# Expert choice in three parts of 16 experts, two of them beside the experts' products

## The chip, the cores and the metric

The kernel is one launch on one core of a Trainium2 chip. The metric is the device time of the launch in microseconds. The engines are TensorE (PE), VectorE (DVE), ScalarE (ACT), GpSimd (POOL) and SyncE (SP); the last one only issues transfers. All data are fp32.

## The reference, cut to what matters

Two layers over x of 4 x 1024 rows of 256. Layer 0 is a gated attention and a mixture of 48 experts with expert choice, layer 1 a performer encoder and a feed-forward net. The part that matters here, with T = 4096 rows, E = 48 experts and S = 4 blocks each:

```python
cap = int(1.5 * T / E)                    # 128
logits = xf @ Wr.T                        # T x E
vals, idx = jax.lax.top_k(logits.T, cap)  # 128 best rows for each expert
w = jax.nn.softmax(vals, axis=-1)
h = jax.nn.gelu(jnp.einsum('ecd,esdm->ecsm', xf[idx], W1) + b1[:, None], approximate=False)
y = jnp.einsum('ecsm,esmk->ecsk', h, W2) + b2[:, None]
out = zeros.at[idx.reshape(-1)].add(y * w)
```

Layer 1 needs, beside its inputs, two weights folded with the random features (Wk and Wq times proj), and constants: ln1_b @ W1, the column sums of W2, and shift @ W1 of the last net.

## The kernel before

The stages run one after the other, each in a block of its own; inside a block every engine has its own instruction list, and semaphores set the order between engines. The function `expert_choice` has three blocks.

**The logits stage** (L633 to L768, 100 to 150 us). Eight groups (n) of 512 rows. VectorE updates x, takes statistics (POOL the reciprocal root) and the shift; ScalarE normalises into z; TensorE turns z; ScalarE modulates (`modulate`); TensorE turns back and ScalarE copies the rows (`rows`, L716) into hg, which SP writes to h_dram (L641). TensorE multiplies with Wr, and VectorE's `logits_copy` (L678) puts 48 x 512 logits into `logits`, two groups of 48 partitions with 2048 columns each. On VectorE `logits_copy(n - 2)` stands behind `statistics(n + 1)`; hg and the logits in PSUM have two buffers each.

**The choice** (L770 to L932). VectorE does 16 rounds over `logits` (112 x 2048): MAX8, FIND_INDEX8 and MATCH_REPLACE8 (L825 to L828), eight values a round. Each expert then has two descending lists of 128. TensorE turns both and flips one, and VectorE takes the larger of each pair, which are the 128 best; index and weight follow. Beside this SP loads the first 8 experts and small columns, and TensorE and ScalarE make the two folds (16 transposes L899, a copy, 32 instructions of products L904, a copy L874, a store), the weights of which are loaded in this block, and the three constants (L912, L915, L919).

**The products** (L935 to L1102). A ring of 8 experts' weights. For expert e TensorE does up(e + 1) (32 instructions, L1082), turn(e + 2) of the gathered rows (L1073) and down(e) (16, L1091). VectorE adds b1 over 128 x 1024 (L1053) and b2 (L1064), ScalarE copies the turned rows (L1023), does one GELU over 128 x 1024 (L1027) and weighs y (L1032). POOL gathers rows six experts ahead (L987) and adds y to a sum in DRAM (L999). SP loads expert e + 8 once b2 of e has been added. All run in loops of eight experts.

Of the kernel before, what the change touches and what calls it, by code (L numbers as in the profile page):

```python
# [12 lines left out]
ALU = mybir.AluOpType  # L13
# [4 lines left out]
I32 = mybir.dt.int32  # L18
# [570 lines left out]
TOP = 8  # L589


def expert_choice(nc, mk, g, a):

    HALF = T // 2
    LOW = 64
    ROWS = LOW + E
    with ExitStack() as ctx:
# [6 lines left out]
        weight = t.sb("weight", [P, E])  # L604
        h_dram = nc.dram_tensor("h_dram", (T, D), F32, kind="Internal").ap()
# [10 lines left out]
        with ExitStack() as c2:  # L616
            r = Maker(nc, c2)
            logits = r.sb("logits", [ROWS, HALF])

            with ExitStack() as c3:  # L620
                t = Maker(nc, c3)
                z, hg = t.sb("z", [P, 2, G, D]), t.sb("hg", [P, 2, G, D])
                hT = t.sb("hT", [P, 2, KD, GT])
                wrT = t.sb("wrT", [P, KD, E])
                st, mv, var, rstd, shift = (t.sb("st1", [P, G, 6]), t.sb("mv1", [P, 2, G, 2]), t.sb("var1", [P, 2, G]), t.sb("rstd1", [P, 2, G]),
                                            t.sb("shift1", [P, 2, G]))
                tp, lp, back = t.ps("tp1", [P, 2, KD, GT]), t.ps("lp1", [P, 2, GT]), t.ps("back1", [P, G, D])
                own, blank, var_ready, rstd_ready, shift_ready = (mk.sem("ec_dve"), mk.sem("ec_blank"), mk.sem("ec_var"), mk.sem("ec_rstd"),
                                                                  mk.sem("ec_shift"))
                z_ready, turned, hT_ready, back_done, h_ready = (mk.sem("ec_z"), mk.sem("ec_turned"), mk.sem("ec_hT"), mk.sem("ec_back"),  # L630
                                                                 mk.sem("ec_h"))
                logits_done, logits_out, wrT_done, wrT_copied = (mk.sem("ec_logits"), mk.sem("ec_logits_out"), mk.sem("ec_wrT"),
                                                                 mk.sem("ec_wrT_copied"))  # L633
                h_out = [mk.sem("ec_h_out0"), mk.sem("ec_h_out1")]
                part = lambda n: slice(LOW * (n // (NG // 2)), LOW * (n // (NG // 2)) + E)
                with nc.Block() as block:
                    @block.sync
                    def _(sp):
                        for n in range(NG):
                            sp.wait_ge(h_ready, n + 1)  # L640
                            sp.dma_start(h_dram[n * GT:(n + 1) * GT, :].rearrange("(t p) d -> p t d", p=P), hg[:, n % 2]).then_inc(h_out[n % 2], 16)  # L641
                        for k in range(2):
                            sp.wait_ge(h_out[k], 16 * (NG // 2))

                    @block.gpsimd
                    def _(pool):
                        pool.memset(logits[32:64, :], LOWEST).then_inc(blank, 1)
                        pool.wait_ge(blank, 1)
                        for n in range(NG):
                            pool.wait_ge(var_ready, n + 1)  # L650
                            if n >= 2:
                                pool.wait_ge(shift_ready, n - 1)
                            rsqrt_rows(pool, rstd[:, n % 2], var[:, n % 2], g.minus_half, G, rstd_ready)

                    @block.vector
                    def _(dve):
                        v = Steps(dve, own)

# [1734 lines left out]
```

## Time and profile before

| | |
|---|---|
| time, three runs | 1721.37, 1722.84, 1730.1 us, median 1722.84 |
| the profiled execution | 1728.49 us, its span 1726.7 us |
| TensorE busy in the span | 1495.2 us, 87% |
| VectorE | 1171.5 us, 68% |
| ScalarE, POOL | 642.8 us and 526.5 us, 37% and 30% |
| granted TensorE clock, mean | 0.924 of full |

Shares over the whole span mix stages with different limits: one reads the stretch that a change touches. Busy times overlap across engines. The span begins with the first and ends with the last instruction of the profile, and the rest of the execution's time lies around it.

### The profile page before, as it was taken

Reading aid. Unit: us, or ns where it says so; the run is one execution under the profiler, and the core shown is the slowest. Engines: PE = TensorE matmul, PEld = TensorE weight load, DVE = VectorE, ACT = ScalarE, POOL = GpSimd, SP = SyncE. Lnnn points to the kernel's source line nnn. Section 1 sums busy time; section 2 is a strip of 40 time slices with the busy share of each in tenths; the row PEclk is TensorE's granted clock in tenths of the full one; section 3 lists DMA queues with packets and bytes.
Section 4 is the critical chain, followed back from the end, with each engine's and each line's share of the span. In section 5 each row is a group of like instructions: output and inputs, shape, how many; then the busy total and the mean of one; then the engine's idle time right before and its main releaser. Section 6 shows DMA issues by size and latency. Waiting matters only on the chain. (4 is left out here: it accounts for less than half of the span.)

```text
span 1726.7 us, 22918 instructions
## 1 busy us (share of the span) xinstructions
PE 1495.2 (87%) x8460; PEld 1248.3 (72%) x8460; DVE 1171.5 (68%) x1867; ACT 642.8 (37%) x947; POOL 526.5 (30%) x511
## 2 busy tenths in 40 slices
PE   8874236999998399999997999999976999989997
PEld 6442236999998266666655788888865888878887
DVE  6576992222222668877737878787856987798886
ACT  1044102333333122222222333333326776766774
POOL 2410003555554012222224200000003555546666
PEclk7788657999999599999998999999997999999999
DMA  5516903999993301112113000000012100000001
GB/s 195 220 37 235 320 6 98 296 292 297 297 291 58 123 25 37 37 37 62 36 49 110 0 25 25 25 25 25 13 52 98 50 25 14 1 1 25 13 25 37
DMA packets 127835, 157.16 MB, mean 91 GB/s; under 512 B 13952, under 2 KB 95992, under 8 KB 126720
## 3 DMA queue, kind: packets, MB, share of 16 engines
q1 hardware_dynamic: 115952, 138.12, 24.6%
q0 software_dynamic: 9216, 12.59, 3.6%
q10 hardware_dynamic: 2576, 5.26, 0.8%
q8 instruction: 54, 0.88, 0.2%
q14 instruction: 37, 0.30, 0.1%
HBM read 122.35 MB, written 33.60 MB: 90 GB/s over the span
## 5 line engine op out<-in xcount | busy, mean ns | idle before, releaser
L2031 POOL TENSOR_TENSOR ff_hid_lo<-ff_hid,ff_hid_hi 128x512 fp32r<-128x512 f32 x128 | 176.0, 1376 | 161.1 <-ACT ff_hid_hi L1940 161.1
L1082 PE MATMUL h_ps<-xT,w 128*128 128x128 f32 x1536 | 192.9, 284 | 1.0 <-ACT xT L1023 1.0
L1082 PEld LDWEIGHTS h_ps<-xT,w 128*128 128x128 f32 x1536 | 186.3, 197 | 1.6 <-issue 0.9
L1053 DVE TENSOR_TENSOR pre<-h_ps,b1T 128x1024 f32<-128x1024 f32 x48 | 58.8, 1225 | 176.4 <-PE h_ps L1082 176.4
L2315 PE MATMUL ff_down<-ff_w_hi,ff_hid_hi 128*128 128x256 f32 x512 | 147.7, 288 | 4.1 <-POOL ff_hid_lo L2031 3.6
L2317 PE MATMUL ff_down<-ff_w_hi,ff_hid_lo 128*128 128x256 f32 x512 | 146.4, 286 | 0.0
L2316 PE MATMUL ff_down<-ff_w_lo,ff_hid_hi 128*128 128x256 f32 x512 | 146.2, 286 | 0.0
L116 POOL TENSOR_TENSOR ff_rstd<-ff_var,minus_half 128x4 f32<-128x4 f32 x24 | 25.5, 1061 | 358.9 <-DVE ff_var L111 356.6
L1117 PE MATMUL k_ring<-w_hi,hT_hi 128*128 128x512 f32 x256 | 118.7, 464 | 9.5 <-DVE hT_lo L1277 6.4
L1458 PE MATMUL k_acc<-wide_rows,hk 128*128 128x512 f32 x256 | 119.7, 599 | 4.3 <-ACT wide_rows L1402 4.3
L1117 PE MATMUL q_ring<-w_hi,hT_hi 128*128 128x512 f32 x256 | 109.8, 429 | 9.8 <-PEq L99 6.8
L1747 PE MATMUL q_out_ps<-kv_sums,wide_rows 128*128 128x256 f32 x512 | 115.5, 379 | 0.0
L2301 PE MATMUL ff_ring<-ff_rowsT_hi,ff_w_hi 128*128 128x512 f32 x256 | 103.0, 402 | 8.4 <-DVE ff_rowsT_lo L2089 3.6
L2315 PEld LDWEIGHTS ff_down<-ff_w_hi,ff_hid_hi 128*128 128x128 f32 x512 | 99.1, 194 | 10.6 <-POOL ff_hid_lo L2031 5.0
L1747 PEld LDWEIGHTS q_out_ps<-kv_sums,wide_rows 128*128 128x128 f32 x512 | 96.3, 190 | 13.2
L2302 PE MATMUL ff_ring<-ff_rowsT_lo,ff_w_hi 128*128 128x512 f32 x256 | 102.4, 400 | 0.0
L2316 PEld LDWEIGHTS ff_down<-ff_w_lo,ff_hid_hi 128*128 128x128 f32 x512 | 99.3, 194 | 4.2
L1119 PE MATMUL k_ring<-w_hi,hT_lo 128*128 128x512 f32 x256 | 102.2, 399 | 0.0
L1118 PE MATMUL k_ring<-w_lo,hT_hi 128*128 128x512 f32 x256 | 101.8, 398 | 0.0
L1119 PE MATMUL q_ring<-w_hi,hT_lo 128*128 128x512 f32 x256 | 101.7, 397 | 0.0
L1118 PE MATMUL q_ring<-w_lo,hT_hi 128*128 128x512 f32 x256 | 101.6, 397 | 0.0
L1393 ACT ACTIVATE k_squares<-k_ring 128x1024 f32<-128x1024 f32 x32 | 32.8, 1025 | 182.3 <-PE k_ring L1119 182.3
(374 smaller groups left out, 3537.4 us busy)
## 6 DMA issues: line engine op xcount, KB each, us to landing
w<-in_L_ffn_W_dram SPq DMA_DIRECT2D x48, 1024.0 KB, 5.8
w<-in_L_ffn_W_dram SPq DMA_DIRECT2D x48, 256.0 KB, 6.1
expert_sum_dram<-f_zero SPq DMA_DIRECT2D x8, 1024.0 KB, 14.9
b_rows<-in_L_ffn_b_dram SPq DMA_DIRECT2D x48, 128.0 KB, 8.8
x<-in_L_attn_x_dram SPq DMA_DIRECT2D x4, 1024.0 KB, 12.4
h_dram<-hg SPq DMA_DIRECT2D x8, 512.0 KB, 2.9
hk<-expert_sum_dram SPq DMA_DIRECT2D x8, 512.0 KB, 4.4
hT_hi<-expert_sum_dram SPq DMA_DIRECT2D x8, 512.0 KB, 5.2
```

The source lines that it names most:

```text
L1082: last = pe.matmul(h_ps[:, q % 2, s * KD + c, :], w1[:, q, s, k, c::KD], xT[:, q % 2, k, :], start=(k == 0), stop=(k == KD - 1))
L1117: pe.matmul(out, x[0], w[0][:, cols], start=start, stop=False)
L1118: pe.matmul(out, x[0], w[1][:, cols], start=False, stop=False)
L1119: return pe.matmul(out, x[1], w[0][:, cols], start=False, stop=stop)
L1458: last = pe.matmul(acc[:, k, cols], hk[:, n % KV_RING, j, k * P:(k + 1) * P], dash[:, n % 2, j, cols], start=(j == 0), stop=(j == G - 1))
L1747: last = pe.matmul(out_ps[:, i % 2, 0:D], qnT[:, i % 2, c, :], kv_out(i // TB)[:, c, :], start=(c == 0), stop=(c == CH - 1))
L2031: pool.tensor_tensor(hid_lo[:, m % PARTS, :], hid[:, m % WHOLES, :], hid_hi[:, m % PARTS, :].bitcast(F32), ALU.subtract).then_inc(part_low, 1)
L2301: pe.matmul(slot(u), high[:, d, cols], x[:, n % 2, d, :], start=(d == 0), stop=False)
L2302: pe.matmul(slot(u), high[:, d, cols], x_low[:, n % 2, d, :], start=False, stop=False)
L2315: pe.matmul(into, hid_hi[:, m % PARTS, tile], high[:, c, :], start=(c == 0 and j % 2 == 0), stop=False)
L2316: pe.matmul(into, hid_hi[:, m % PARTS, tile], low[:, c, :], start=False, stop=False)
L2317: last = pe.matmul(into, hid_lo[:, m % PARTS, tile], high[:, c, :], start=False, stop=(c == CF - 1 and j % 2 == 1))
```

## The change

- The experts are chosen in three parts of 16 (`PHASES`). The logits of part p lie in `lists[:, p, :]`, 128 partitions x 512: partition 16 n + i holds expert i of the part over the rows of group n. Each part takes 16 rounds over 128 x 512, gives 8 descending lists of 128 for each expert, and finds the 128th value by merging them as bitonic lists on 16 partitions (`send_lists`, `sort_steps`), without indices. Then the lists' entries above that value are counted, their places found by a product with triangles (`rank`), and indices and weights are moved to them by seven conditional shifts (`move`) and joined by products.
- Part 0 runs before the first product, and the first 8 rounds of part 1 too. The rest of part 1 and part 2 are cut into slots behind `add(e)` on VectorE, with their TensorE steps ahead of `down(e)`. Iterations 0 to 3 and 12 to 19 have two rounds each, iterations 4 to 13 and 20 to 29 the merging.
- The logits go through `stage` and three transfers a group (`spread`) to their partitions.
- In the logits stage SP also loads the weights of folds and constants (1 MB each, into ring slots 3 to 7), and experts 0 and 1. Choice and products are one block, so two blocks are left.
- b1 becomes the bias of eight GELUs of 128 x 128; VectorE's addition is gone. The loops are unrolled. Rows are gathered 5 experts ahead. x_ps and y_ps take one bank each, and `down(e)` waits for `add(e - 1)`. The sums over W2 are made by POOL (seven additions) and one product.

```diff
+PHASES = 3
+EP = E // PHASES
+LISTS = P // EP
+AHEAD, STARTS, ROUND_SLOTS, COUNTS_AT = 8, (0, 0, 12), (0, 4, 8), (0, 8, 24)
+FOLD_SLOT, ELU_SLOT, WAVE_SLOT = 3, 5, 7
...
+                    def ahead(n):
+                        if n == 0:
+                            for k in range(2):
+                                sp.dma_start(proj2[:, k, :], a["L1_attn_proj"]).then_inc(proj_in, 16)
+                        if n < 2:
+                            sp.dma_start(w_raw[n], a[("L1_attn_Wk", "L1_attn_Wq")[n]]...).then_inc(fold_in[n], 16)
...
+                        if 5 <= n < NG - 1:
+                            load_expert(sp, n - 5, n - 5)
+                    def spread(n):
+                        sp.wait_ge(logits_out, n + 1)
+                        for i in range(PHASES):
+                            sp.dma_start(lists[n * EP:(n + 1) * EP, i, :], stage[i * EP:(i + 1) * EP, n % 2, :]).then_inc(lists_in[n % 2], 16)
+                    for n in range(NG):
+                        sp.wait_ge(h_ready, n + 1)
+                        sp.dma_start(h_dram[n * GT:(n + 1) * GT, :]..., hg[:, n % 2]).then_inc(h_out[n % 2], 16)
+                        ahead(n)
+                        if n >= 2:
+                            spread(n - 2)
...
+                    def logits_copy(n):
+                        dve.wait_ge(logits_done, n + 1)
+                        if n >= 2:
+                            dve.wait_ge(lists_in[n % 2], 16 * PHASES * (n // 2))
+                        dve.tensor_copy(stage[:, n % 2, :], lp[0:E, n % 2, :]).then_inc(logits_out, 1)
...
-                        act.activation(act_h[:, q % 2], pre[:, q % 2], ACT.Gelu).then_inc(gelu_done, 1)
+                        for s in range(S):
+                            for c in range(KD):
+                                last = act.activation(act_h[:, e % 2, s * KD + c, :], h_ps[:, e % 2, s * KD + c, :], ACT.Gelu,
+                                                      bias=b1T[:, e * S + s, c:c + 1])
...
+                    def sort_steps(lists_left, first, count):
+                        for i in range(first, first + count):
+                            j = P >> (i + 1)
+                            of, to = (order[:, (i + x) % 2, 0:lists_left, :]... for x in range(2))
+                            v.mark(dve.tensor_tensor(to[:, :, 0, :], of[:, :, 0, :], of[:, :, 1, :], ALU.max))
+                            v.mark(dve.tensor_tensor(to[:, :, 1, :], of[:, :, 0, :], of[:, :, 1, :], ALU.min))
+                            v.sync()
...
+                    def move(lists, first, count):
+                        for i in range(first, first + count):
+                            of, to, step = lists[:, i % 2, :], lists[:, (i + 1) % 2, :], 1 << i
+                            v(dve.tensor_scalar(to, of, bits[:, 1, i:i + 1], None, ALU.mult))
+                            v(dve.scalar_tensor_tensor(to[:, step:], of[:, 0:P - step], bits[:, 0, i:i + 1], to[:, step:], ALU.mult, ALU.add))
...
+                    rounds(0, 0, CAP // TOP)
+                    listed(0)
+                    turn_back(0)
+                    first_level(0)
+                    sort_steps(4, 0, 7)
+                    second_level()
+                    sort_steps(2, 0, 7)
+                    last_level()
+                    counts(0)
+                    placed(0)
+                    move(moved, 0, 7)
+                    dve.sem_inc(shifted, 1)
+                    weights_in(0)
+                    indices(0)
+                    move(moved_w, 0, 7)
+                    dve.sem_inc(valued, 1)
+                    rounds(1, 0, AHEAD)
+                    weights(0)
+                    for e in range(E):
+                        add(e)
+                        for p in range(1, PHASES):
+                            k = e - STARTS[p]
+                            if 0 <= k < ROUND_SLOTS[p]:
+                                rounds(p, CAP // TOP - 2 * (ROUND_SLOTS[p] - k), 2)
+                            if k == ROUND_SLOTS[p] - 1:
+                                listed(p)
+                            if e == COUNTS_AT[p] - 4:
+                                turn_back(p)
...
+                    for e in range(E):
+                        if e + 1 < E:
+                            up(e + 1)
+                        if e + 2 < E:
+                            turn(e + 2)
+                        for p in range(1, PHASES):
+                            if e == COUNTS_AT[p] - 4:
+                                turn_top(p)
+                            if e == COUNTS_AT[p] - 3:
+                                send_lists(p)
+                            if e == COUNTS_AT[p] + 1:
+                                rank(p)
+                            if e == COUNTS_AT[p] + 3:
+                                join_indices(p)
+                            if e == COUNTS_AT[p] + 5:
+                                join_weights(p)
+                        down(e)
```

The rest of the slots: `first_level` with three sorting steps behind add(5), four and `second_level` behind add(6), seven and `last_level` behind add(7), `counts` behind add(8), `placed` and three shifts behind add(9), four behind add(10), `indices`, `weights_in` and four shifts behind add(11), three behind add(12), `weights` behind add(13); for part 2 the same 16 experts later. Before the first product TensorE's list is turn_top(0), send_lists(0), the third constant, send_edge(0), rank(0), join_indices(0), join_weights(0), turn(0), up(0).

## Rows read from the trace of the kernel before

**Rows 1.** windows of two stretches: busy us of each engine, TensorE's clock, DMA share, GB/s.
```profile
150.00:270.00 120.00, 35.38 (x189) 32.49 (x189) 113.47 (x93) 8.73 (x10) 0.61 (x3) 0.61 0.52 180
...
300.00:400.00 100.00, 100.00 (x867) 100.00 (x866) 28.11 (x35) 33.77 (x53) 54.70 (x87) 1.00 1.02 295
```

**Rows 2.** timeline of VectorE, two starts of a round: start us, duration us, instruction.
```profile
150.20 2.29 DVE L825 MAX8 top<-logits 112x8 f32<-112x2048 f32 x1 [1.90 <-PEq L636]
...
157.31 2.29 DVE L825 MAX8 top<-logits 112x8 f32<-112x2048 f32 x1
```

**Rows 3.** groups of VectorE by shape: busy us, mean ns of one, idle before.
```profile
L1053 DVE TENSOR_TENSOR pre<-h_ps,b1T 128x1024 f32<-128x1024 f32 x48 | 58.8, 1225 | 176.4 <-PE h_ps L1082 176.4
...
L1064 DVE TENSOR_TENSOR biased_y<-y_ps,b_rows 128x256 f32<-128x256 f32 x48 | 20.4, 425 | 32.1 <-PE y_ps L1091 32.1
...
L678 DVE COPY logits<-lp 48x512 f32<-48x512 f32 x8 | 5.5, 689 | 13.8 <-PE lp L741 13.7
...
L315 DVE TENSOR_TENSOR masked<-coef,eye_b 128x128 f32<-128x128 f32 x2 | 0.6, 292 | 0.1
```

**Rows 4.** timeline from the last round to the first product.
```profile
262.94 0.39 DVE L833 COPY both<-rank_ps 128x224 f32<-128x224 f32 x1 [0.79 <-PE rank_ps L924]
...
263.45 0.66 PE L927 MATMUL peak_ps<-both,rank 128*128 128x48 f32 x2 [0.54 <-DVEq L834]
...
271.32 1.29 POOL L987 DMA_INDIRECT xg<-h_dram,slot  x1 [0.46 <-POOL pool_spare L980]
...
274.53 0.70 PE L1073 MATMUL x_ps<-ident,xg 128*128 128x128 f32 x2 [5.64 <-DMA xg<-h_dram,slot]
...
275.80 0.55 PE L1082 MATMUL h_ps<-xT,w 128*128 128x128 f32 x1 [0.56 <-ACT xT L1023]
```

**Rows 5.** timeline of TensorE, two neighbouring experts.
```profile
334.13 3.99 PE L1082 MATMUL h_ps<-xT,w 128*128 128x128 f32 x32
...
339.91 3.99 PE L1082 MATMUL h_ps<-xT,w 128*128 128x128 f32 x32
```

**Rows 6.** timeline at the second expert's down().
```profile
291.94 1.90 PE L1091 MATMUL y_ps<-w,act_h 128*128 128x64 f32 x16
```

**Rows 7.** timeline of the logits stage.
```profile
121.25 2.07 ACT L699 ACTIVATE z<-x,shift,rstd 128x256 f32<-128x256 f32 x4
...
123.22 1.00 ACT L716 ACTIVATE hg<-back 128x1024 f32<-128x1024 f32 x1
...
125.55 0.68 DVE L678 COPY logits<-lp 48x512 f32<-48x512 f32 x1 [0.17 <-PE lp L741]
```

**Rows 8.** DMA issues of the whole span: count, KB each, us from issue to landing.
```profile
w<-in_L_ffn_W_dram SPq DMA_DIRECT2D x48, 1024.0 KB, 5.8
...
b_rows<-in_L_ffn_b_dram SPq DMA_DIRECT2D x48, 128.0 KB, 8.8
...
xg<-h_dram,slot POOLq DMA_INDIRECT x48, 5.5
...
ff_b_elu<-in_L_attn_b_dram SPq DMA_DIRECT2D x1, 4.0 KB, 12.0
...
ff_wav<-in_L_ffn_b_dram SPq DMA_DIRECT2D x1, 4.0 KB, 2.6
```

**Rows 9.** timeline of one fold pass.
```profile
188.80 3.67 PE L899 MATMUL fold_ps<-ident,w_raw 128*128 128x128 f32 x16 [13.69 <-DMA w_raw<-in_L_attn_Wq_dram]
...
199.70 1.88 ACT L874 ACTIVATE w_fold<-fold_ps 128x2048 f32<-128x2048 f32 x1 [5.30 <-PE fold_ps L904]
```

**Rows 10.** groups of ScalarE by shape.
```profile
L1032 ACT ACTIVATE y<-biased_y,weight 128x256 f32<-128x256 f32 x48 | 24.4, 508 | 6.1 <-DVE biased_y L1064 2.6
L1023 ACT ACTIVATE xT<-x_ps 128x256 f32<-128x256 f32 x48 | 18.4, 383 | 149.9 <-PE x_ps L1073 149.9
...
L699 ACT ACTIVATE z<-x,shift,rstd 128x256 f32<-128x256 f32 x32 | 16.6, 592 | 1.1 <-DVE shift L672 1.1
...
L1027 ACT ACT_TABLE_LOAD x1 | 1.3, 1283 | 0.0
```

More of the change, by code:

```diff
@@ new lines, in _, with carry, scatter @@
+                    steps = iter(range(1, 3 * E))
+                    def carry():
+                        carry_wait(next(steps))
+                    def scatter(e):
+                        pool.wait_ge(y_ready, e + 1 + 2)
+                        carry()
+                        pool.indirect_dma_start(out=sums[e % 2], out_offset=bass.IndirectOffsetOnAxis(ap=slot[:, e % XG], axis=0),
+                                                in_=y[:, e % 2, :], in_offset=None, compute_op=ALU.add).then_inc(added[e % 2], 16)
@@ L1047, in _, with exps @@
-                    bodies(act, body)
+                        act.activation(y[:, e % 2, :], biased_y[:, e % 2, :], ACT.Copy, scale=weight[:, e:e + 1]).then_inc(y_ready, 1)
+                    def exps(p):
+                        act.wait_ge(edge_ready, p + 1)
+                        act.activation(ex[:], top[:], ACT.Exp, bias=edge[:, 1:2]).then_inc(top_exp, 1)
+                    act.wait_ge(fold_turned, 1)
+                    act.wait_ge(blank, 1)
+                    for i in range(2):
+                        rows = slice(i * DH, (i + 1) * DH)
+                        last = act.activation(features[rows, i * MF:(i + 1) * MF], fold_ps[rows, 0:MF], ACT.Copy, scale=DN)
@@ L1050, in _ @@
                 def _(dve):
[L1051 to L1061 removed]
+                    v = Steps(dve, own)
@@ new lines, in rounds, with listed @@
+                    def rounds(p, first, count):
+                        for n in range(first, first + count):
+                            cols = slice(n * TOP, (n + 1) * TOP)
+                            v(dve.max(top[:, cols], lists[:, p, :]))
+                            v(dve.max_index(at[:, cols], top[:, cols], lists[:, p, :]))
+                            if n < CAP // TOP - 1:
+                                v(dve.match_replace(lists[:, p, :], top[:, cols], lists[:, p, :], LOWEST))
+                    def listed(p):
+                        dve.sem_inc(found, 1)
+                        v(dve.tensor_copy(at_f[:], at[:]))
@@ new lines, in _ @@
+                    turn_top(0)
+                    send_lists(0)
+                    pe.wait_ge(wave_w_in, 16)
+                    for c in range(CF):
+                        for k in range(KD):
+                            last = pe.matmul(fold_ps[:, 1024 + c * B:1024 + (c + 1) * B], w_wave[:, k, c * P:(c + 1) * P], g.shift_col[:, k, :],
+                                             start=(k == 0), stop=(k == KD - 1))
+                    last.then_inc(wave_consts, 1)
+                    send_edge(0)
```

825 lines of the change are left out of this document (440 added, 385 removed).

## The prediction

> **What bounds the kernel now.** I read the windows by stage first. Between the logits and the experts' products lie 120 us in which VectorE works 113 us, TensorE a third of the time and at half clock for much of it. That is the choice. From 300 us on, the products keep TensorE at 100.00 of 100 us at full clock, with the DMA engines at their limit too (share 1.02) [rows 1]. So in the choice only VectorE counts, and in the products only TensorE. The timeline of the choice shows a round: three passes over 112x2048, 7.11 us from one MAX8 to the next, 2.37 us a pass with its gap [rows 2]. There are 16 rounds, without the last MATCH_REPLACE: 47 passes or 111.4 us, from 150.2 to 261.6 us. From there to the first product (275.80 us) 14.2 us go by, in handshakes, the stage's end and the first gather [rows 4]. In the products one expert takes 5.78 us [rows 5].
>
> The sum below is made against the span, 1726.7 us; that execution took 1728.49 us, 5.7 us above the median 1722.84. The difference is taken off the median.
>
> **1. Shorter passes before the first product.** Each partition now holds 512 logits instead of 2048, and only a third of the experts has to be chosen first. The trace shows no MAX8 of 512. Two VectorE passes out of PSUM, 256 and 512 columns wide, take 425 and 689 ns, 1.03 ns a column [rows 3]; 1536 columns fewer make 2.37 into 0.79 us. 47 passes: 37.1 us, 74.3 us less. Bounds: a quarter of 2.37 (no fixed cost) gives 27.8 us, 0.9 us a pass 42.
>
> **2. A longer way from the last round to the first product.** The lists of 8 partitions must be merged. From the end of the rounds, F: transpose and turn back 1.4 us (the exchange with TensorE costs 0.79 [rows 4]); eight products of a 16-column list with 128 columns, 16 instructions, between 0.33 us (0.66 for two that stand alone, cold [rows 4]) and 0.125 (warm, part 4), I take 0.24, 4.0; first level 1.6 (689 + 2 x 425 ns); seven sorting steps of two 256-column operations, 0.9 each, 6.3; second level 0.6; seven steps of two 128-column ones (292 ns [rows 3]), 0.63 each, 4.4; last level 1.0; the edge through TensorE 0.8; counts 1.2; ranks 1.1; 14 small operations of placed() at 0.17 to 0.2 us, 3.0; 14 of move() over 128 columns at 0.29, 4.0; join_indices 0.8, the copy 0.2. Indices at F + 30.4. The gather adds 0.9 to its issue and 3.2 to landing (271.32 to 274.53 [rows 4]). But join_weights stands ahead of turn(0) on TensorE, and waits for a second move() of 4.0: turn(0) at F + 35.5, up(0) at F + 36.8. Against 14.2: +22.6 us. If TensorE is warm and short operations overlap, +17; if each handshake costs 0.5 more, +28.
>
> **3. The logits stage.** Beside each h block, SP now issues 1 MB of weights (two experts, 1.4 MB each, at n = 5 and 6), and then three transfers of spread(n - 2). logits_copy(n) waits for these on VectorE, and behind it stand update, statistics and shift of the following blocks, for which ScalarE waits. In the trace logits_copy(2) starts at 125.55, while rows(2) has just ended at 124.22 [rows 7]; only then can h, weights and spread(0) be issued. When does spread land? A 4 KB load took 12.0 us behind others and 2.6 us on an empty queue; 1 MB takes 5.8 us, a broadcast of b2 8.8 us [rows 8]. I take it that spread lands behind its neighbours: 6.3 us after rows(n), 10 after an expert's load. Step by step: copy(2) at 131 instead of 125.6; shift(5) 5.7 us late; R(4), the end of rows(4), at 136.8 instead of 133.5; copy(4) at 143; R(5) at 141.4; copy(5), behind expert 0's b2, at 152; copy(6), behind expert 1's, at 158; spread(7) issued by 161.4 and landed by 163.5. The first MAX8 starts there instead of at 150.2: +13.3 us. If small transfers land in 2.6 us, +6.4; if SP's issues are held up by a full queue as well, +20. The Trainium skill ("DMA: Bandwidth & Descriptors", Why a DMA increments its semaphore by 16 and not by 1 and the section on ordering of hardware queues) says that a completion increment lands only after every earlier write of that DMA engine. By it the stage costs the 13.3; without it the 6.4. The row of the 4 KB load agrees with it.
>
> Off the path: the weights of the folds are in place when the choice starts. One fold pass took 12.8 us (188.80 to 201.58 [rows 9]), so two, the projection and the constants take some 35 us from 161.7 and end 3 us before the rounds (200.6). POOL's seven sums replace eight products and are done by then. If the rounds come out shorter, this chain takes their place. In the loops the hardware queue loses nothing: the same 1.4 MB an expert.
>
> **4. The products.** The bias leaves VectorE (58.8 us in all [rows 3]) and becomes part of eight GELUs of 128x128. Neither was on the path, so nothing is gained. TensorE gains instructions, and it is the bound: per later part 1 transpose, 16 for the lists, and 2, 4, 2 and 4, 29 at 0.125 us (3.99 us for 32 [rows 5]), 3.6 us; two parts 7.2. The rest is waits. y_ps now lies in one bank, so down(e) waits for add(e-1), which stands behind VectorE's rounds. Before the loop VectorE does 8 rounds of part 1 (19.0 us) and weights(0), so add(0) ends at F + 54.6. down(1) would start 16.1 us after up(0) (291.94 - 275.80 [rows 4, 6]), at F + 52.9: 1.8 us. Each slot then has two rounds, 4.74 us, and add, 0.42: 5.2 of 5.78, which fits. turn_top(1) in iteration 4 waits for the end of slot 3: TensorE is ready at F + 72.8, the list at F + 75.1, 2.5 us. In part 2 the same wait is 5.3 - 4.3 = 1.1 us. An Exp in iterations 8 and 24 brings two table loads of 1.28 us [rows 10] into ScalarE; GELU is then 0.4 us late, 0.8 in all. Sum: 7.2 + 1.8 + 2.5 + 1.1 + 0.8 = 13.4 us. Gathers five ahead have over two experts' time, 11.6 us, to land, and land in 5.5 [rows 8], so LEAD costs nothing. Unrolled loops: TensorE has no idle time between 300 and 400 us, where two passes of the loop of eight experts end [rows 1], so nothing is gained. The Trainium skill ("Runtime: NRT & Kernel Launch", Instruction fetch mechanics) says that a taken branch can cost a fetch and straight code none; by it the loop would win something. The full window speaks against a gain here.
>
> **Sum.** -74.3 + 22.6 + 13.3 + 13.4 = -25.0 us: the median goes to 1697.8, I say 1698.
>
> **The rivals.**
> - Spread lands in 2.6 us whatever is in the queue (the other 4 KB row): the stage costs 6.4 instead of 13.3, 1691 us. Chance 0.20.
> - The products lose more: every expert 0.3 us longer because add and turn_top hang on VectorE's slots with 0.6 us of room. 48 x 0.3 = 14.4: 1712 us. For it: 5.2 of 5.78 is an estimate over unseen passes (rounds of 2.65 us fill the slot). Against: between two down() TensorE has 5.78 - 1.90 = 3.9 us of other work [rows 5, 6], in which add may be late. Chance 0.16.
> - The folds end after the rounds: rounds at the lower bound (27.8 us) would end at 191.3, the constants at 197; TensorE then sets the start, 1694 us. Chance 0.06.
> - Slower than before: ScalarE becomes the bound of the products. It does one copy (383 ns), weigh (508 ns) [rows 10] and eight GELUs of g. With 0.5 us of gaps, 5.78 us are full at g = 0.55 us; at 0.72, 7.15 us an expert, the loop loses 66 us: 1763. It decides against the change from g = 0.64 on. For it: a 128x256 pass with scale and bias takes 592 ns on the average [rows 10]. Against: four of them lie within 2.07 us [rows 7], so 0.52 each, and half the columns cost less; I take 0.32. Chance 0.05.
> - The change does what it says and no more is late: the rest.
>
> **How the numbers follow.** My forecast 0.53 (own range 1688 to 1708), the others as above. The median of this kernel can be told from no change from about 0.5% on, 8.6 us. Faster: the forecast, the first and third rival, and two thirds of the second: 0.53 + 0.20 + 0.06 + 0.09 = 0.88; same 0.07; slower 0.05. The range leaves out the best bounds (all at once -55 us) and the slower case: 1680 to 1713.
>
> **What the profile would show.** MAX8 128x512 at 0.7 us; first MAX8 near 163 us; up(0) near 237 us; logits copies with waits for DMA of some 5 us; an expert still 5.78 us; TensorE idle before turn_top. Wrong I am most likely in the logits stage (spread's landing) and in the count of small steps after the rounds.

## The result, and the profile after

The changed kernel takes 1698.22 us (median of 4 runs, 1696.27 to 1701.64), the kernel before in the same comparison 1722.57 us: ratio 0.9846, 95% interval 0.982 to 0.9873. The forecast was 1698. Measured in the traces, its four terms sum to -28.1 us instead of -25.0, with errors of 0.9 to 3.3 us in each.

The timeline of the changed kernel at the borders of its stages (columns as in [rows 2]: start, duration, engine, line, operation, and in brackets the idle time before it and its releaser):

```profile
97.43 1.40 DVE L105 BATCH_NORM_STATS2 st<-x 128x6 f32<-128x256 f32 x4 [1.42 <-PEq L99]
...
163.05 0.69 DVE L995 MAX8 top<-lists 128x8 f32<-128x512 f32 x1
...
165.37 0.69 DVE L995 MAX8 top<-lists 128x8 f32<-128x512 f32 x1
...
167.68 0.70 DVE L995 MAX8 top<-lists 128x8 f32<-128x512 f32 x1
...
199.37 0.47 PE L1172 MATMUL pick_ps<-ident,top 128*128 128x128 f32 x1 [8.32 <-DVEq L1001]
...
234.60 6.58 PE L1214 MATMUL h_ps<-xT,w 128*128 128x128 f32 x32 [0.56 <-ACT xT L934]
...
525.77 0.42 DVE L1105 TENSOR_TENSOR biased_y<-y_ps,b_rows 128x256 f32<-128x256 f32 x1 [2.15 <-PE y_ps L1225]
```

A round takes 2.31 us (165.37 to 167.68) instead of 7.11, and the line of turn_top says that TensorE, done with its folds, idled 8.32 us for VectorE. By such starts the two traces compare as follows (us; the span of the changed kernel is 1694.5, its clock 0.934):

| stage | before | after | difference | forecast |
|---|---|---|---|---|
| up to the first BN_STATS of the logits stage | 100.35 | 97.43 | -2.9 | 0 |
| logits stage, to the first MAX8 | 49.85 | 65.62 | +15.8 | +13.3 |
| 47 passes | 111.4 | 36.2 | -75.2 | -74.3 |
| last round to up(0) | 14.2 | 35.3 | +21.2 | +22.6 |
| products, up(0) to the last add | 281.1 | 291.2 | +10.1 | +13.4 |
| the rest | 1169.8 | 1168.7 | -1.1 | 0 |

The spans differ by 32.2 us, the medians by 24.35. The 7.9 us between are scatter: the profiled execution of the kernel before took 5.9 us more than its median, that of the changed kernel 1.95 us less. Of them 2.9 lie in the first row, a stage that both kernels share (looked at in experiment 1).

**The logits stage.** Answers for the logits copy and the list transfers of the changed kernel (the second figure in "26.1, 6" is the number of waits):

```profile
L708 DVE COPY logits_rows<-lp x8: 682/683/683, 112.5 to 158.6; 48x512 f32<-48x512 f32 x8
  DMA lists<-logits_rows: 26.1, 6
L664 SPq DMA_DIRECT2D lists<-logits_rows x24: 507/592/1160, 121.5 to 160.9; - x24
DMA to landing us min/median/max: 1.9/5.3/6.3
```

VectorE stood 26.1 us in six waits for lists. The last h copy (hg) ends 52.4 us after the first BN_STATS; in the kernel before it was 46.4. So the waits behind which update, statistics and shift stood cost 6.0 us. The other 9.8 us lie behind that copy: 13.2 us to the first MAX8 instead of 3.4. SyncE's queue in the changed kernel shows them:

```profile
145.96 0.37 SPq L668 DMA_DIRECT2D h_dram<-hg  x1
146.37 0.51 SPq L615 DMA_DIRECT2D w<-in_L_ffn_W_dram  x1
146.92 0.90 SPq L616 DMA_DIRECT2D w<-in_L_ffn_W_dram  x1
147.87 0.94 SPq L617 DMA_DIRECT2D b_rows<-in_L_ffn_b_dram  x1
148.84 2.46 SPq L664 DMA_DIRECT2D lists<-logits_rows  x3
151.35 0.58 SPq L668 DMA_DIRECT2D h_dram<-hg  x1
151.97 9.48 SPq L664 DMA_DIRECT2D lists<-logits_rows  x9
```

The last h block is issued at 151.35, 1.5 us after its copy ended, for SP is still busy with expert 1 and spread(4). The last row merges three spreads, and a wait lies inside it. VectorE's copy of block 6, the last six issues in a narrower window, and SP's waits from 145 to 165 us (total, times, longest):

```profile
157.07 0.68 DVE L708 COPY logits_rows<-lp 48x512 f32<-48x512 f32 x1 [7.25 <-DMA lists<-logits_rows]
...
157.78 3.67 SPq L664 DMA_DIRECT2D lists<-logits_rows  x6
...
SPq L664 <- DVE logits_rows L708: 4.6, 2, 3.5
```

So three issues take 2.26 us, then SP waits 3.5 us for the copy of block 6, which itself waited 7.25 us for its staging buffer, that is for the landing of spread(4); the last six issues take 3.67 us.

**The products.** TensorE's timeline around expert 4 of the changed kernel:

```profile
263.76 1.90 PE L1225 MATMUL y_ps<-w,act_h 128*128 128x64 f32 x16
...
270.68 0.33 PE L1172 MATMUL pick_ps<-ident,top 128*128 128x128 f32 x1 [0.98 <-DVEq L1001]
270.84 1.91 PE L1225 MATMUL y_ps<-w,act_h 128*128 128x64 f32 x16
272.59 3.99 PE L1214 MATMUL h_ps<-xT,w 128*128 128x128 f32 x32
...
276.73 0.39 PE L1178 MATMUL pick_ps<-ident,topT 128*16 128x128 f32 x2
...
278.27 0.38 PE L1178 MATMUL pick_ps<-flip,topT 128*16 128x128 f32 x2
278.58 2.00 PE L1225 MATMUL y_ps<-w,act_h 128*128 128x64 f32 x16
```

From down to down one expert takes 7.08 us (263.76 to 270.84, with the wait of 0.98 for VectorE's rounds), the next 7.74 (16 list instructions), an expert without side work 5.78 as before [rows 5]. From 300 to 400 us, TensorE works 99.70 of 100 us (it was 100.00 [rows 1]).

### The profile page after: what moved, and what is told of

Its sections match the earlier page's. It is cut to its first block and busy times, and to the rows that moved or that the text cites. A ratio compares the mean times of both kernels' runs of the same rounds, so it can differ in the third digit from the quotient of the medians.

```text
span 1694.5 us, 23216 instructions
## 1 busy us (share of the span) xinstructions
PE 1501.0 (89%) x8521; PEld 1251.7 (74%) x8521; DVE 1175.3 (69%) x2242; ACT 694.1 (41%) x1289; POOL 533.4 (31%) x519
## 5 line engine op out<-in xcount | busy, mean ns | idle before, releaser
L1105 DVE TENSOR_TENSOR biased_y<-y_ps,b_rows 128x256 f32<-128x256 f32 x48 | 20.4, 425 | 148.0 <-PE y_ps L1225 137.0
L2501 PEld LDWEIGHTS ff_down<-ff_w_hi,ff_hid_hi 128*128 128x128 f32 x512 | 98.6, 193 | 11.2 <-POOL ff_hid_lo L2217 5.0
L1933 PEld LDWEIGHTS q_out_ps<-kv_sums,wide_rows 128*128 128x128 f32 x512 | 96.3, 190 | 13.2
L940 ACT ACTIVATE act_h<-h_ps,b1T 128x128 f32<-128x128 f32 x384 | 104.0, 390 | 2.8 <-PE h_ps L1214 2.7
## 6 DMA issues: line engine op xcount, KB each, us to landing
expert_sum_dram<-f_zero SPq DMA_DIRECT2D x8, 1024.0 KB, 15.4
```

What stands on the lines that cost most here:

```text
L940: last = act.activation(act_h[:, e % 2, s * KD + c, :], h_ps[:, e % 2, s * KD + c, :], ACT.Gelu, bias=b1T[:, e * S + s, c:c + 1])
L1933: last = pe.matmul(out_ps[:, i % 2, 0:D], qnT[:, i % 2, c, :], kv_out(i // TB)[:, c, :], start=(c == 0), stop=(c == CH - 1))
L2501: pe.matmul(into, hid_hi[:, m % PARTS, tile], high[:, c, :], start=(c == 0 and j % 2 == 0), stop=False)
```

## The experiments

Times are medians. The kernel before was timed again beside each group of runs, and its median came out between 1722.57 and 1724.83 us, so kernels of different groups are best compared by their ratios. "Stage" is from the first BN_STATS to the first MAX8, "products" from up(0) to the last add, both as in the table.

**1. The kernel before once more.**

> The kernel before, unchanged, profiled a second time. Its first profiled execution took 1728.49 us, 5.9 us over its median, and reached the first BN_STATS of the logits stage 2.9 us later than the changed kernel did, in a stage that the change doesn't touch. Theory: that is scatter between executions, so this one shows the logits stage from some 97.5 us on, a logits stage of 49.9 us and products of 281 us again, and a time near 1722. Rival: the change moves the stage in front too (its layout in memory, its instruction stream); then the stage starts at 100.3 again, whatever the time.

1727.2 us for this one execution, beside a median of 1722.91. First BN_STATS at 100.61, logits stage 49.1, products 281.7. The stages repeat within 0.8 us, so the table's differences hold to about that. The start of the stage is the rival's (100.3), not the theory's (97.5), but the rival's reason doesn't hold for every kernel either: of the twelve profiles of the changed kernel and its variants below, ten have their first BN_STATS between 96.9 and 98.1 us and two at 100.2. The front stage thus has two lengths some 2.7 us apart, and the changed kernel's family shows both; the kernel before was seen at the long one twice. Whether it also has the short one stays open, and so does the place of the other 5 us of scatter.

**2. The logits stage: who makes the lists late?** Four edits of the changed kernel.

```
e1_spread_first
-                        ahead(n)
                         if n >= 2:
                             spread(n - 2)
+                        ahead(n)
e2_stage4
-            stage = t.sb("logits_rows", [E, 2, GT])
+            stage = t.sb("logits_rows", [E, 4, GT])
-                        if n >= 2:
-                            dve.wait_ge(lists_in[n % 2], 16 * PHASES * (n // 2))
+                        if n >= 4:
+                            dve.wait_ge(lists_in[n % 4], 16 * PHASES * (n // 4))
e3_no_ahead
-                        ahead(n)
+                    (start of the next block: the same loads, experts 0 to 2, then the columns)
e11_spread_pool
-                            spread(n - 2)      (on SP)
+                        if n >= 3:
+                            spread(n - 3)      (on GpSimd, behind rsqrt_rows of block n)
```

> The changed kernel, but SP issues the three transfers of spread(n - 2) ahead of the weights of block n, not behind them. Theory (a list lands behind the loads that were issued before it): each list then follows only the 0.5 MB h block and lands about 4 to 5 us after R(n), the end of the h copy, instead of 8 to 11; the logits copies wait 1 to 2 us each instead of up to 7.3, the stage takes 54 to 58 us instead of 65.6, and the time is some 10 us under 1698: 1688. Rival (SP's own issue times and a fixed latency of some 5 us set the landing): only the issue of one or two loads, 1 to 2 us, goes; the stage takes 63 to 64 us and the time is 1696.

> The changed kernel with four staging buffers for the logits instead of two, so that logits_copy(n) waits for spread(n - 4) and not for spread(n - 2). Theory (the wait of VectorE for the lists holds back update and statistics behind it): spread(n - 4) has landed by the time of the copy, the waits go, R(7) falls from 149.9 to about 140 us on the clock of the changed kernel, and the last lists still land behind expert 1's load: stage 55 to 58 us, time 1689. Rival (the stage is held by the DMA engines, which move 5 MB of weights and 4 MB of h in it): h writes and lists come as late as before, ScalarE waits for the h buffers in place of VectorE for the lists, and the stage stays at 63 to 66 us, time 1697.

> The changed kernel, but all weights for folds, constants and the experts 0 and 1 are issued at the start of the next stage instead of in the logits stage. Theory: without them the logits stage takes about 53 us (three small lists a block remain), 12 us less; the fold chain starts some 5 us after the stage begins, at 157, and takes 35 us; it ends at about 192, 5 us behind the rounds (187), so 7 to 8 of the 12 us are kept: 1690. Rival (the loads were not what made the stage long; the lists' own latency was): the stage takes 62 us or more, and the later fold chain makes it slower than the changed kernel: 1700 or more.

> The changed kernel, but the lists are sent from GpSimd's queue instead of SP's; loads, buffers and everything else as they are. Theory (a list lands late because it stands behind 1 MB of weights in the same queue): from a queue of its own it lands 2 to 2.5 us after its issue, the copies wait less than 2 us each, the h copies end 47 us after the first BN_STATS and the stage takes 54 to 56 us: 1687. Rival (all queues share the 16 DMA engines, which the loads keep full, so another queue doesn't help): lists land 5 us after their issue as before, and the stage takes 62 us or more: 1695 or more.

| run | us | ratio to before, interval | stage | to the end of the last h copy | from there to MAX8 | list, issue to landing (median) |
|---|---|---|---|---|---|---|
| changed kernel | 1698.22 | 0.9846 (0.982 to 0.9873) | 65.6 | 52.4 | 13.2 | 5.3 |
| e1_spread_first | 1694.73 | 0.9841 (0.9815 to 0.9867) | 61.3 | 48.4 | 12.9 | 3.9 |
| e2_stage4 | 1688.27 | 0.9793 (0.9775 to 0.9811) | 57.5 | 46.4 | 11.2 | 4.8 |
| e3_no_ahead | 1698.97 | 0.9866 (0.9845 to 0.9888) | 55.1 | 47.0 | 8.1 | 2.4 |
| e11_spread_pool | 1688.21 | 0.9788 (0.9773 to 0.9803) | 56.5 | 45.4 | 11.1 | 5.0 |

By their ratios e2 and e11 are faster than the changed kernel, while e1 and e3 can't be told from it by the time (the intervals overlap).

The last column answers the question of the landing. Without loads a list lands 2.4 us after its issue, with them 5.3: the loads cost 2.9 us a list. But my account of how was wrong. From GpSimd's own queue, which carries no weights, the list lands after 5.0 us too. GpSimd's timeline in this run, and the answer for its transfers' line:

```profile
126.73 1.51 POOL L673 DMA_DIRECT2D lists<-logits_rows  x3
...
136.01 1.44 POOL L673 DMA_DIRECT2D lists<-logits_rows  x3 [3.13 <-DVE logits_rows L708]
140.66 1.43 POOL L673 DMA_DIRECT2D lists<-logits_rows  x3 [3.21 <-DVE logits_rows L708]
144.14 1.44 POOL L673 DMA_DIRECT2D lists<-logits_rows  x3 [2.05 <-DVE logits_rows L708]
```

```profile
DMA to landing us min/median/max: 3.1/5.0/6.4
```

So most of the delay is not the place in SP's queue; what both queues share are the DMA engines. Two findings on SP's own queue fit this: the changed kernel's last six lists, issued from 157.8 us on with the DMA share at 0.17, landed after 1.9 to 2.0 us, and with the lists issued ahead of their block's load (e1) the median was 3.9. One thing stays open: a list from GpSimd without the loads was not run. Its shortest landing was 3.1 us, against 1.9 on SP, so a part of the 5.0 may be that queue's own. The engines are busier in this stage than before it was changed; windows of the changed kernel (PEclk, DMA share and GB/s at the end):

```profile
120.00:130.00 10.00, 7.65 (x40) 3.78 (x38) 3.00 (x14) 6.26 (x10) 1.01 (x1) 1.00 1.01 347
140.00:150.00 10.00, 6.89 (x36) 3.47 (x35) 1.43 (x3) 6.90 (x10) 0.00 (x0) 1.00 0.99 287
```

The same windows of the kernel before have shares of 0.34 and 0.37. Yet the run from GpSimd's queue had a landing of 5.0 and lost all waits of the copies. What it changed is when a list is issued: SP's program held spread(n - 2) behind its wait for h block n, though its copy was long done (copy(0) ended at 113.2, spread(0) went out at 121.5), and each of the three issues costs SP 0.5 to 1.2 us. The list waits were thus SP's order, plus its issue times, plus a landing lengthened by the loads; one long link less was enough. The rival was right on the landing and wrong on the time. The Trainium skill ("DMA: Bandwidth & Descriptors", Issuing engines are not separate DMA queues) says both halves of this: transfers from any engine run on the same DMA engines, and another issuing engine saves only the time of issuing, which it calls small beside the transfer. The runs agree on the first half. On the second, the issues were not small here: the three of a block took SP 2.0 to 2.9 us, beside a landing of 5.3. In this run the stage's end is set by something else. SP had issued the last h block by 144.2, expert 1's 1.4 MB just ahead of it, and then waited for the h writes; the next block began at 152.50:

```profile
SPq L666 <- DMA h_dram<-hg: 7.8, 1, 7.8
```

Four buffers take back all 6.0 us of the first part and 2.0 of the second; stage and time came as forecast, though the last h copy was forecast to come 10 us earlier. SP's nine last issues now follow each other without a wait:

```profile
149.90 6.17 SPq L664 DMA_DIRECT2D lists<-logits_rows  x9
```

Spread first got 4.3 us, between the two forecasts: a list still goes out only behind the wait for h(n). How long the copies wait says little by itself. Their waits sum to 26.1, 21.7 and 15.3 us in the changed kernel, e1 and e3, and the last h copy came 6.0, 2.0 and 0.6 us later than in the kernel before.

**3. Why does the run without loads gain nothing?** It shortened the stage by 10.5 us, more than the other three, and took 1698.97 us. Its queue and TensorE:

```profile
175.44 0.67 SPq L617 DMA_DIRECT2D b_rows<-in_L_ffn_b_dram  x1
176.16 1.91 SPq L854 DMA_DIRECT2D ff_b_elu<-in_L_attn_b_dram  x1
178.10 6.46 SPq L856 DMA_DIRECT2D ff_ln_col<-in_L_attn_ln_g_dram  x1
...
190.62 0.58 SPq L862 DMA_DIRECT2D ff_wav<-uantum_weights_imag_dram  x1
```

```profile
173.43 3.84 PE L1251 MATMUL h_ps<-features,w_turned 128*128 128x128 f32 x32 [1.97 <-ACT w_turned L967]
193.78 6.96 PE L1259 MATMUL h_ps<-ff_ln_col,w 128*128 128x1 f32 x32 [16.51 <-issue]
...
201.60 0.42 PE L1178 MATMUL pick_ps<-ident,top 128*128 128x128 f32 x1
```

The folds were done at 177. The constants, which stand ahead of turn_top(0) on TensorE, then waited 16.51 us. The row names no releaser, but the wait ends 2.6 us after SP issued the last of the column loads, which stood behind 4.2 MB of experts. The rounds were over at 188.8 (152.57 + 36.2), turn_top came at 201.6. I tested that by the order alone:

```
e10_columns_first (against e3_no_ahead)
-                    for e in range(FOLD_SLOT):
-                        load_expert(sp, e, e)
                     ... (column loads)
+                    for e in range(FOLD_SLOT):
+                        load_expert(sp, e, e)
```

> The run without loads in the logits stage once more, but the small column loads are issued ahead of the experts 0 to 2, not behind them. Theory (there the constants waited until 193.8 us for columns queued behind 4.2 MB of experts, and TensorE reached turn_top 12.8 us after the rounds' end): the constants end before the rounds do, turn_top follows the rounds at once, up(0) comes 71.6 us after the first MAX8 again, and the time is 12 us less than there: 1687. Rival (the folds' own weights are late too, or the experts' weights now come after up(0) is ready): half of that, 1692 or more.

1689.61 us, ratio 0.98 (0.9785 to 0.9815), 9.4 us less than the run before by the medians and 11 by the ratios, of 12 forecast; stage 55.8. turn_top came at 194.40, still 4.6 us behind the rounds (153.62 + 36.2 = 189.8), instead of 12.8. The order of the queue was the main cause. The rest is TensorE's: its fold products took 6.75 and 6.71 us here instead of 3.84, at a mean granted clock of 0.61 from 159 to 191 us (0.82 in the run above; why it was lower isn't shown). This is the third rival of the prediction, the folds that end after the rounds, seen at work.

It was closer than one profile of the changed kernel says. The run with six gathers (e4, below) changes nothing in this stretch; its products of the folds took 6.78 and 6.74 us at a mean granted clock of 0.59 (166 to 203 us), and of the cover of 8.32 us this was left:

```profile
202.56 0.47 PE L1172 MATMUL pick_ps<-ident,top 128*128 128x128 f32 x1 [0.90 <-DVEq L1001]
```

**4. The products.** Four edits:

```
e4_lead6
-            XG, LEAD = 8, 5
+            XG, LEAD = 8, 6
e5_bias_dve
-       for s, c: act.activation(act_h[:, e % 2, s * KD + c, :], h_ps[:, e % 2, s * KD + c, :], ACT.Gelu, bias=...)
+       act.activation(act_h[:, e % 2], act_h[:, e % 2], ACT.Gelu)
+       dve, ahead of add(e): act_h[:, (e + 1) % 2] = h_ps[:, (e + 1) % 2] + b1T, 128x1024
e6_no_side_work
-       rounds, listed, ... weights of p = 1, 2 and TensorE's and ScalarE's steps for them
-       index[:, e:e + 1], weight[:, e:e + 1]
+       index[:, e % EP:e % EP + 1], weight[:, e % EP:e % EP + 1]
e7_pe_order
-       join_weights(0); turn(0); up(0); turn(1)          -       turn_top(p); down(e)
+       turn(0); up(0); join_weights(0); turn(1)          +       down(e); turn_top(p)
```

> The changed kernel with six gathers ahead again instead of five (LEAD = 6). Theory (a gather has two experts' time and more to land, and lands in about half of it, so its lead costs nothing): products 291 us, 1698, the ratio to before as that of the changed kernel, 0.985. Rival (the fifth gather came too late for some expert, and part of the 10 us that the products grew is a wait of TensorE for a gather): the products shrink by 1 to 3 us. Against six: gather(16) would stand in GpSimd's queue before index 16 exists, and could hold the scatter of expert 11; that would show as one longer interval near expert 12, at most 2 us.

1697.68 us, ratio 0.9838 (0.981 to 0.9866), products 291.2. Lead costs nothing, at five or six.

> The changed kernel without the choice of parts 1 and 2: the experts 16 to 47 take the indices and weights of the experts 0 to 15, so rounds, sorting, lists and moves of two thirds of the experts are left out, and so are TensorE's 58 instructions for them. Theory (all of the 10.1 us that the products grew is side work: TensorE's own instructions and its waits for VectorE): the products take 281 us again, 5.78 us each, and the time is 1688. Rival (gathers five ahead, the split GELU or the unrolled loops cost something by themselves): an interval stays over 5.78 us, and the products take 284 us or more.

1685.92 us for one execution of this kernel, which leaves out the choice of parts 1 and 2; products 281.5, and every interval 5.78 but the last two. So unrolled loops, the lead and the split GELU cost nothing, and win nothing: of the 10.1 us that the products grew, 9.65 are side work (291.17 - 281.52).

> The changed kernel with the bias b1 back on VectorE: one addition of 128x1024 an expert (1.22 us, 58.8 us in all) ahead of each add, and one GELU of 128x1024 in place of eight of 128x128. Theory (in the 12 slots with rounds VectorE has 5.1 us of work in 5.78, so it can't take 1.22 us more; outside of them the bias costs nothing): the 12 slots take 6.4 to 7 us instead of 5.8 to 7, which is 5 to 12 us more in the products, none after expert 20; 1706. Rival (the chain up, bias, GELU, down is longer than the 3.9 us that TensorE has between two downs when VectorE is in a round): each of the 12 slots waits for a whole round more, 2.3 us, 28 us in all: 1726, slower than before. Third (VectorE has the room): 1698.

1720.87 us, ratio 0.9975 (0.9961 to 0.999): almost the whole gain of the change is gone. Products 314.2, 23 us more, nearer to the rival in size, but neither theory had the place. VectorE and TensorE of this run:

```profile
243.45 1.22 DVE L1102 TENSOR_TENSOR act_h<-h_ps,b1T 128x1024 f32<-128x1024 f32 x1 [8.88 <-PE h_ps L1221]
244.59 0.68 DVE L993 MAX8 top<-lists 128x8 f32<-128x512 f32 x1
...
263.60 1.22 DVE L1102 TENSOR_TENSOR act_h<-h_ps,b1T 128x1024 f32<-128x1024 f32 x1
264.75 0.41 DVE L1109 TENSOR_TENSOR biased_y<-y_ps,b_rows 128x256 f32<-128x256 f32 x1
```

```profile
253.83 0.39 PE L1212 MATMUL x_ps<-ident,xg 128*128 128x128 f32 x2
265.97 3.68 PE L1232 MATMUL y_ps<-w,act_h 128*128 128x64 f32 x16 [11.76 <-ACT act_h L940]
269.44 5.74 PE L1221 MATMUL h_ps<-xT,w 128*128 128x128 f32 x32
```

bias(1) stands behind eight rounds: the first two intervals take 15.0 us more, 11.76 of them the wait, the rest a down of 3.68 us instead of 1.90 and an up of 5.74 instead of 3.98 behind it (granted clock 0.50 from 266 to 269.4 us, 0.65 to 275). The five slots 14 to 18 cost 0.3 to 0.5 us each, the last slot with rounds and the one behind it 6.0. The bias inside the GELU gains nothing by itself; it is what lets the side work be cheap in this order. An order with bias(1) among the eight rounds wasn't run, so most of the 23 us may be the price of the place and not of the addition.

> The changed kernel with two of TensorE's steps moved: join_weights(0) behind up(0) instead of ahead of turn(0), and turn_top(1), turn_top(2) behind the down of their iteration instead of ahead of it. Theory (turn(0) waited for the second move(), 1.9 us after its gather had landed at the latest; turn_top waited 1.3 us for VectorE's rounds): up(0) comes 1 to 2 us earlier, counted from the last round, and the intervals before down(4) and down(20) lose 1 us each: 3 us in all, 1695. Rival (turn(0) is held by the gather, whose landing is at about the same time, and the waits in the loop only move to y_biased): nothing, 1698.

1696.82 us, ratio 0.9838 (0.9816 to 0.9861). up(0) came 69.6 us after the first MAX8 as forecast, and both waits of turn_top went. But the products took 292.8 us. TensorE of this run, and windows of it:

```profile
252.54 1.97 PE L1225 MATMUL y_ps<-w,act_h 128*128 128x64 f32 x16 [2.13 <-DVE biased_y L1105]
254.35 5.51 PE L1214 MATMUL h_ps<-xT,w 128*128 128x128 f32 x32
```

```profile
252.50:254.50 2.00, 1.96 (x17) 1.99 (x18) 1.93 (x5) 2.00 (x8) 1.33 (x3) 1.00 0.42 72
254.50:258.00 3.50, 3.50 (x20) 3.50 (x19) 3.33 (x9) 1.28 (x4) 1.95 (x5) 0.54 1.00 314
```

down(1) waited 2.13 us for add(0), which stands behind the eight rounds of part 1, and then the granted clock was 0.54 for 3.5 us (close to the lower of TensorE's two levels, 1.2 GHz, from full clock before), so that the next up took 5.51 us instead of 3.98. Together 3.7 us, nearly all that the new order had won. Neither forecast had the second part.

**5. Both together.**

```
e8_logits
+            stage [E, NG, GT], no wait of the copies; spread(n - 2) ahead of ahead(n); experts 0 to 2
+            behind the column loads; ScalarE issues spread(6) and a third of spread(7)
e9_all (against e8_logits): the edit of e7_pe_order and
-AHEAD, STARTS, ROUND_SLOTS, COUNTS_AT = 8, (0, 0, 12), (0, 4, 8), (0, 8, 24)
+AHEAD, STARTS, ROUND_SLOTS, COUNTS_AT = 6, (0, 0, 12), (0, 5, 8), (0, 9, 24)
```

> The changed kernel with the logits stage freed: eight staging buffers (no copy waits for lists), spread(n - 2) ahead of the weights of block n, the experts 0 and 1 loaded in the next stage behind the small column loads, and the six list transfers of the last two blocks shared by SP's and ScalarE's queues. Theory (the 15.8 us that the stage grew are 6.7 us of VectorE's waits for lists and 9.8 us between the last h copy and the first MAX8, in which SP issues nine lists behind expert 1's load): the h copies end 46.4 us after the first BN_STATS as in the kernel before, the first MAX8 follows 5 us later; stage 51.5 to 53 us, 13 us less than the changed kernel, 1685. Rival (the weights and column loads that move behind the stage hold TensorE's folds or constants, as in the run without loads in the logits stage): turn_top waits for them and the time is 1690 or more.

1684.51 us, ratio 0.9772 (0.9759 to 0.9786). Stage 52.4: h copies end 46.6 us in, MAX8 5.8 us later, and turn_top waits for VectorE 8.35 us, not for the constants. The theory holds in each part. The kernel is 13.7 us faster than the changed one by the medians, some 13 by the ratios; the stage gives 13.2.

> The kernel of the run before with TensorE's order of the earlier run (join_weights(0) behind up(0), turn_top behind down) and six instead of eight rounds of part 1 ahead of the first add, so that part 1 takes five slots and its later steps come one expert later. Theory (the first adds held down(1) in the run with the new order, so its gain was lost there; with two rounds less, 4.7 us, they don't): up(0) 69.6 us after the first MAX8 instead of 71.5, turn_top without a wait, products 288 to 289 us instead of 291; 4 us less than the kernel of the run before: 1681. Rival (VectorE's slots of 5 us leave 0.8 us of room in 5.78, so the adds of the first experts stay what the downs wait for, wherever the rounds stand): no more than the 1.9 us of up(0), or nothing: 1683 to 1685.

1683.25 us, ratio 0.9759 (0.9744 to 0.9775): lowest of all, though not to be told from the run before. The first five intervals are 5.78 us each, so add(0) no longer holds down(1). But the loss came back at part 1's new place:

```profile
316.03 0.50 PE L1204 MATMUL x_ps<-ident,xg 128*128 128x128 f32 x2 [0.32 <-DMA xg<-h_dram,slot]
317.50 0.39 PE L1198 MATMUL pick_ps<-by_expert,moved_weights 128*128 128x16 f32 x2 [0.97 <-DVEq L1163]
...
319.79 5.52 PE L1213 MATMUL h_ps<-xT,w 128*128 128x128 f32 x32
```

Two short waits of 1.3 us, and again an up of 5.52 (granted clock 0.66 from 319.5 to 324.5): the two intervals with join_indices and join_weights take 15.4 us instead of 12.0 in the run before. Products 292.1. The time is the rival's, its reason isn't: the adds were not what the downs waited for.

## Why the prediction was right

**The number.** That the median met 1698 within 1 us is luck in part. The terms were off by -0.9, -1.4, +2.5 and -3.3 us, together 3.1 us too little gain by the traces, and the median moved by only 24.35 us of those 28.1, within an interval of some 22 to 31 us. MAX8 came at 163.05 us, near the forecast 163, only because the stage in front was 2.9 us shorter and the logits stage 2.5 longer. In the chances, two thirds of the second rival's 0.16 are 0.11, not 0.09.

**Step 1, the passes.** 0.77 us a pass instead of 0.79, 36.2 us instead of 37.1. The line through two unlike operations of 256 and 512 columns gave the pass over 512 within 3%.

**Step 2, the way to the first product.** 35.3 us instead of 36.8. A product of the lists took 0.21 cold (0.24 assumed), the first level to the last 11.9 us (13.9 assumed: a 16x256 operation takes 0.41 us, and pairs overlap), a step of move() 0.67 to 0.71 from start to start instead of 0.58. turn(0) did wait for join_weights, 1.9 us by the run that moved it.

**Step 3, the logits stage.** This term was under-sized: 15.8 instead of 13.3. What was off in it is "spread lands behind its neighbours: 6.3 us after rows(n), 10 after an expert's load". The landings were 8.1, 9.0 and 8.1 us after the h copy in blocks 2 to 4, and 9.5 and 11.1 behind the two experts. The middle case had no price for SP's issues, three a block at 2 to 3 us (slow issues stood only in its bound of +20). At the end three spreads take 9.48 us: 5.9 of issues, and 3.5 in which SP waits for the copy of block 6 and that copy for a list. The mechanism was half right: lists are late through the loads, but not by their place in SP's queue, since from GpSimd's own queue they landed hardly sooner. The rule of the Trainium skill quoted there ("DMA: Bandwidth & Descriptors", Why a DMA increments its semaphore by 16 and not by 1) speaks of the writes of a DMA engine. That fits a delay that another queue doesn't escape; my reading of it, as a matter of the neighbours in one queue, is what the run refuted. The first rival (2.6 us whatever is in the queue) is out: a median of 2.4 us was seen only without the loads.

**Step 3, off the path.** The folds were expected to end 3 us before the rounds and left 8.3 us in the changed kernel's profile, but 0.9 in another kernel with the same stretch, at a lower granted clock (0.59 from 166 to 203 us instead of 0.73 from 163 to 200). Two runs showed what this cover hides: with late loads it is gone, and TensorE is 4.6 and 12.8 us late.

**Step 4, the products.** Over-sized: 10.1 instead of 13.4. TensorE waits for turn_top 0.98 us in part 1 and 0.3 in part 2 (2.5 and 1.1 assumed), down(1) came 0.3 us late instead of 1.8, and no interval shows the 0.8 us put down for table loads. The instructions' 7.2 us were about right: of the 9.65, 8.1 remain when these waits are taken off (9.65 - 1.3 - 0.3). The GELU of 128x128 takes 0.26 us from start to start, below the 0.32 assumed, so ScalarE never became the bound. "Neither was on the path, so nothing is gained" holds for the kernel before, and needs the addition of the bias run: in the changed kernel the addition on VectorE, ahead of each add, is on the path, for 23 us in the order that was run. Unrolled loops won nothing (intervals of 5.78 in the run without side work), as the full window had said. By the rule of the Trainium skill ("Runtime: NRT & Kernel Launch", Instruction fetch mechanics) taken branches can cost a fetch; the loops of this kernel show no such cost (5.78 us an expert with them and without).

The second rival, every expert 0.3 us longer, didn't happen: from expert 30 on all intervals are 5.78.

## What to carry to other kernels

When a queue is given more to carry, count for each small transfer behind it three things apart: how long its issue waits for the program's order, the issue times of all that stand ahead (0.5 to 1.2 us each here), and a landing that was twice as long here with the DMA engines full. A merged row of issues can hide a wait: nine issues in 9.48 us were 5.9 us of issues. A staging buffer for each block, at 2 KB a partition, takes all three off the path for every block but the last ones.

A cover has to be counted down whenever the covered stage is made shorter: the run that took all loads out of the logits stage won 10.5 us there and lost them to constants whose columns of a few KB stood behind 4.2 MB. And work removed from an engine with room may gain nothing and still be what another part of the change stands on; only undoing it alone shows that.

## What the runs showed of the hardware that was not expected

- A list of 32 KB landed 2.4 us (median) after its issue in the run without loads, with the DMA share at 0.41 (120 to 140 us), and 5.0 to 5.3 us with it near 1, from SyncE's queue and from GpSimd's.
- The issue of a list on SyncE's queue took a median of 0.59 us with the loads and without them (0.51 to 1.16 in the changed kernel, 0.51 to 0.93 in the run without loads).
- In the products short waits of TensorE can cost more than themselves: behind 2.13 us, and in another run behind 1.3, the granted clock was 0.54 and 0.66 for the next 3.5 to 5 us, and an up took 1.5 us more. In the changed kernel the wait of 0.98 had no such effect (the next up took 3.99), with spread first the same wait, 0.99, had (0.62 from 268.5 to 273 us, interval 9.26 instead of 7.74). What decides it stays open.
